# Megakernel on one core: weights loaded in order of use, x loaded turned, and a last stage that adds the two expert results on TensorE, takes its small statistics for two batches at once and holds four consecutive tokens per partition

## What is computed

```python
x = _layernorm(x + _L0_attn_ref(x, ...))   # state-space block: x @ W_in, conv over 4 taps, pw_kernel, 8-state scan
x = _layernorm(x + _L0_ffn_ref(x, w))      # x @ sign(w).T
x = _layernorm(x + _L1_attn_ref(x, ...))   # gated linear attention, 16 heads of 64
x = _layernorm(x + _L1_ffn_ref(x, ...))    # 8 experts, each token takes its best 2, hidden size 512
...
def _layernorm(x, axis=-1, eps=1e-05):
    m = jnp.mean(x, axis=axis, keepdims=True)
    v = jnp.var(x, axis=axis, keepdims=True)
    return (x - m) / jnp.sqrt(v + eps)
```

## Time and profile before

| | |
|---|---|
| median of 3 runs | 2472.59 us (2466.28 to 2479.43) |
| profiled execution: time, span | 2474.75 us, 2472.9 us |
| busy over the span | PE 85%, weight loads 63%, DVE 79%, ACT 58%, POOL 33% |
| 0 to 20 us | PE 0.00, DVE 2.01, ACT 1.28 us busy; DMA busy 0.84 |
| a round (521.3 to 636.4 us) | 115.1 us: PE 103.96, DVE 99.83, ACT 77.85, POOL 39.13 us busy; PE clock 1.00 |
| 2420 to 2440 us | PE 0, DVE 19.14, ACT 9.71, POOL 16.53 us busy; PE clock 0.50; DMA 0.81 busy, 229 GB/s |

### The profile page before, as it was taken

The page is one execution under the profiler, slowest core; times in us unless marked ns, Lnnn a source line. Parts: engine busy times, 40 slices in busy tenths (PEclk is TensorE's granted clock), DMA queues, the critical chain, the costliest instruction groups (busy, mean ns, idle before and its releaser), DMA issues. The chain is left out here.

```text
span 2472.9 us, 52605 instructions
## 1 busy us (share of the span) xinstructions
PE 2107.4 (85%) x15800; PEld 1560.8 (63%) x15929; DVE 1962.8 (79%) x3681; ACT 1427.6 (58%) x3256; POOL 808.0 (33%) x1060
## 2 busy tenths in 40 slices
PE   4389898989989898989898989899889849999980
PEld 1147565656657565657575656566566749999980
DVE  2787989798988888888988897989885447777768
ACT  2366766666667675666767666666655413333334
POOL 0111424141415141423324241414141333333337
PEclk9699999999999999999999999999989969999995
DMA  3452424152433324243424241524230042122117
GB/s 118 103 126 61 107 69 117 50 124 61 111 86 81 102 64 102 65 114 78 108 69 101 68 116 51 124 60 111 72 92 14 30 151 59 55 60 59 55 52 196
DMA packets 160526, 212.88 MB, mean 86 GB/s; under 512 B 20296, under 2 KB 97104, under 8 KB 160064
## 3 DMA queue, kind: packets, MB, share of 16 engines
q1 hardware_dynamic: 138192, 144.20, 19.7%
q0 software_dynamic: 22272, 67.92, 13.4%
HBM read 134.71 MB, written 28.08 MB: 66 GB/s over the span
## 5 line engine op out<-in xcount | busy, mean ns | idle before, releaser
L1432 DVE TENSOR_TENSOR_SCAN hs<-decay,push 128x512 f32<-128x512 f32 x256 | 320.1, 1272 | 7.1
L1184 ACT ACTIVATE S<-banks,fall_tok 128x128 f32<-128x128 f32 x1024 | 278.8, 385 | 27.7 <-PE banks L816 27.4
L1003 PE MATMUL banks<-rowsT,w_here 128*128 128x128 f32 x2176 | 269.6, 278 | 6.5 <-DVE w_here L1774 6.5
L1003 PEld LDWEIGHTS banks<-rowsT,w_here 128*128 128x128 f32 x2176 | 256.0, 193 | 10.1 <-issue 9.1
L1853 POOL DMA_DIRECT2D y<-ch x96 | 88.1, 918 | 477.2 <-DVE ch L1440 374.5
L1944 POOL TENSOR_TENSOR qd<-q,q_fall 128x512 f32<-128x512 f32 x96 | 159.4, 1660 | 208.7 <-ACT chunk_fall L1169 208.7
L1540 DVE TENSOR_TENSOR S<-banks,S 128x512 f32<-128x512 f32 x256 | 167.8, 683 | 64.2 <-PE banks L828 44.9
L1985 POOL DMA_INDIRECT results_scratch<-rows_out,result_to x136 | 132.2, 972 | 241.2 <-ACT rows_out L1310 234.5
L1425 DVE TENSOR_TENSOR push<-du,b_all 128x1024 f32<-128x1024 f32 x128 | 198.1, 1547 | 2.0 <-DMA b_all<-bc_scratch 2.0
L1299 ACT ACTIVATE tanh_h<-banks 128x512 f32<-128x512 f32 x136 | 81.3, 598 | 203.3 <-PE banks L1003 203.3
L1547 DVE SCALAR_TENSOR_TENSOR oT<-tog,banks 128x512 f32<-128x512 f32 x128 | 87.2, 681 | 136.0 <-ACT sq L1152 135.9
(11 more groups left out here) (221 smaller groups left out, 5096.5 us busy)
## 6 DMA issues: line engine op xcount, KB each, us to landing
y<-ch POOLq DMA_DIRECT2D x96, 512.0 KB, 5.5
b_all<-bc_scratch SPq DMA_DIRECT2D x128, 256.0 KB, 3.9
c_all<-bc_scratch SPq DMA_DIRECT2D x128, 256.0 KB, 3.6
q_fall<-fall_scratch SPq DMA_DIRECT2D x192, 128.0 KB, 3.3
rows_in<-rows_scratch SPq DMA_DIRECT2D x136, 66.0 KB
both<-results_scratch SPq DMA_DIRECT2D x32, 256.0 KB, 3.4
w<-w_dram SPq DMA_DIRECT2D x3, 2048.0 KB, 9.6
x_tok<-x_dram SPq DMA_DIRECT2D x16, 256.0 KB, 3.2
```

What stands on the lines that cost most here:

```text
L1003: mm = pe.matmul(bank_h[:, u % 2, n, here], w_here[:, u % 2, n, here], x, start=True, stop=True)
L1184: ins = nc.scalar.activation(S[:, g, here], bank[:, here], ACT.Exp, bias=fall_tok[:, head:head + 1])
L1432: nc.vector.tensor_tensor_scan(hs[:, h, :], decay[:, n % 2, h, :], push[:, h, :], 0.0, ALU.mult, ALU.add).then_inc(s_scan, 1)
```

## The change

1. The list of loads is split in three, each with a semaphore: `conv_loads` (w_inT, taps, pw), then `xT` of batch 0, then seven `front_loads`, then 23 others in the order of use. PE, ACT and DVE wait for each part where it is first used. The preparation of late weights moves on DVE from the start to round 0, behind the convolution's `u1` (`prepare_late`).
2. The tap products use two banks and two tiles in turn.
3. The host passes x turned as well. SP loads it straight into `xT`, once `z1` of the batch before has been multiplied; the transposes, the ACT copy, the tile `x_tok` and the bank use `xT` go, which leaves 97 uses in a round.
4. In the last stage PE adds the two results: two matmuls with the identity into bank `slot`; DVE adds `tokens` to that bank. POOL's addition goes. The seven small steps, the power and the shift are done once for two batches, on 128x8.
5. `tokens`, `both` and `out` hold four consecutive tokens per partition (2 KB runs in DRAM instead of four of 512 B).

```diff
-FRONT = {"xT": 0, "u0": 1, "u1": 2, "xdbl": 3, "dt0": 4, "dt1": 4, "z0": 6, "z1": 6}
+FRONT = {"u0": 1, "u1": 2, "xdbl": 3, "dt0": 4, "dt1": 4, "z0": 6, "z1": 6}
...
-        w_tap = S[:, 1, 2 * P:4 * P].rearrange("p (c n) -> p c n", c=HALVES)
+        w_tap = S[:, 3, :].rearrange("p (s c n) -> p s c n", s=2, c=HALVES)
...
+        tokens_dram = x3_scratch.rearrange("b (p c) d -> b p c d", p=P)
...
-        out_dram = out.rearrange("b (c p) d -> b p c d", p=P)
-        both_dram = results_dram[0:2 * B * T, :].rearrange("(r b c p) d -> r b p c d", r=2, b=B, p=P)
+        out_dram = out.rearrange("b (p c) d -> b p c d", p=P)
+        both_dram = results_dram[0:2 * B * T, :].rearrange("(r b p c) d -> r b p c d", r=2, b=B, p=P)
...
+            for dst, src in conv_loads:
+                sp.dma_start(dst, src).then_inc(s_w_first, 16)
+            sp.dma_start(xT[:, TAPS - 1:TAPS - 1 + T], a["xT"][0]).then_inc(s_x_loaded, 16)
+            for dst, src in front_loads:
+                sp.dma_start(dst, src).then_inc(s_w_front, 16)
...
-                        sp.wait_ge(ring.full_sem("xT"), ring.full_at("xT", n - 1))
-                    sp.dma_start(x_tok[:], x_dram[bass.ds(n, 1)].rearrange("b p c d -> (b p) c d")
-                                 ).then_inc(s_x_loaded, 16)
+                        sp.wait_ge(ring.full_sem("z1"), ring.full_at("z1", n - 1))
+                        sp.dma_start(xT[:, TAPS - 1:TAPS - 1 + T], a["xT"][bass.ds(n, 1)].rearrange("b d t -> (b d) t")
+                                     ).then_inc(s_x_loaded, 16)
...
-                    sp.wait_ge(s_mixed, b + 1)
+                    sp.wait_ge(s_summed, b + 1)
                     load_both(b + FINAL_SLOTS)
...
-                if t >= 1:
-                    pe.wait_ge(s_wconv, t)
+                if t >= 2:
+                    pe.wait_ge(s_wconv, t - 1)
...
+            for b in range(B):
+                slot = b % FINAL_SLOTS
+                after(pe, s_mixed, b - FINAL_SLOTS + 1)
+                pe.wait_ge(s_both[slot], 32 * (b // FINAL_SLOTS + 1))
+                for r in range(2):
+                    mm = pe.matmul(banks[:, slot, :], eye[:], both[:, slot, r].rearrange("p c d -> p (c d)"),
+                                   start=(r == 0), stop=(r == 1))
+                mm.then_inc(s_summed, 1)
...
-                dve.wait_ge(s_added, b + 1)
-                nc.vector.tensor_tensor(final_in[:, slot], both[:, slot, 0], both[:, slot, 1], ALU.add).then_inc(s_mixed, 1)
...
+                dve.wait_ge(s_summed, b + 1)
+                nc.vector.tensor_tensor(final_in[:, slot], banks[:, slot, :].rearrange("p (c d) -> p c d", d=P),
+                                        tokens[:, b * TILES:(b + 1) * TILES, :], ALU.add).then_inc(s_mixed, 1)
...
+            for m in range(B // 2):
+                mix_results(2 * m)
+                mix_results(2 * m + 1)
+                final_deviation(m)
```

More of the change, by code:

```diff
@@ L35 @@
 LN_STEPS = 11
+PAIR_STEPS = 15
 RMS_EPS = float(np.finfo(np.float32).eps)
@@ L311, in build @@
         ones = sb("ones", [P, P])
-        x_tok = sb("x_tok", [P, TILES, P])
         xT = sb("xT", [P, TAPS - 1 + T])
@@ L731, in turn, with convolve @@
                 mm.then_inc(full, 1)
-            def turn_input(n):
+            def convolve(h, n):
                 pe.wait_ge(s_x_loaded, at(n, 16, 16))
-                turn("xT", x_tok, n)
-            def convolve(h, n):
-                bank, full = fill(ring, f"u{h}", n, "xT")
+                bank, full = fill(ring, f"u{h}", n)
                 for t in range(TAPS):
@@ L965, in body @@
             def body(i, j, n):
+                if i is not None and first(i):
+                    pe.wait_ge(s_weights, WEIGHTS)
+                    pe.wait_ge(s_prep_late, PREPARED_LATE)
                 if j is not None:
@@ L1046, in _ @@
                 act.wait_ge(s_wmul, t + 1)
-                nc.scalar.activation(w_conv[:, t, :], ring_banks[:, 0, 0:2 * P], ACT.Copy, scale=0.5
+                nc.scalar.activation(w_conv[:, t, :], ring_banks[:, t % 2, 0:2 * P], ACT.Copy, scale=0.5
                                      ).then_inc(s_wconv, 1)
+            act.wait_ge(s_prep, PREPARED)
             def full(ring, use, it):
@@ L1053, in full @@
                 return ring.bank(use)
-            def turn_input(n):
-                nc.scalar.copy(xT[:, TAPS - 1:TAPS - 1 + T], full(ring, "xT", n)).then_inc(ring.free_sem("xT"), 1)
             def convolved(h, n):
@@ L1256, in body @@
             def body(i, j, n):
+                if i is not None and first(i):
+                    act.wait_ge(s_weights, WEIGHTS)
                 if j is not None:
@@ L1381, in _, with prepare_late @@
             dve.wait_ge(s_prep, PREPARED)
+            def prepare_late():
+                dve.wait_ge(s_weights, WEIGHTS)
+                for w in (w_out, w_k):
+                    nc.vector.tensor_scalar(w[:], w[:], 0.5, None, ALU.mult).then_inc(s_prep_late, 1)
+                for t in range(PAIRS):
+                    nc.vector.tensor_scalar(w_o[:, t, :], w_o[:, t, :], norm_w[:, t:t + 1], 0.5 * HID ** 0.5,
+                                            ALU.mult, ALU.mult).then_inc(s_prep_late, 1)
+                nc.vector.tensor_scalar(w_less, w_ffn[:], 0.0, None, ALU.is_lt).then_inc(s_sign, 1)
+                nc.vector.tensor_scalar(w_sign[:], w_ffn[:], 0.0, None, ALU.is_gt).then_inc(s_sign, 1)
+                dve.wait_ge(s_sign, 2)
+                nc.vector.tensor_tensor(w_sign[:], w_sign[:], w_less, ALU.subtract).then_inc(s_prep_late, 1)
+                nc.vector.tensor_scalar(x3_rows[:, :, TO], token_no[:], float(ALL_TOKENS - T), None, ALU.add
+                                        ).then_inc(s_token_no, 1)
+                dve.wait_ge(s_token_no, 1)
+                dve.wait_ge(s_prep_late, PREPARED_LATE)
             def full(ring, use, it):
@@ L1410, in normalize @@
                                             ALU.subtract, ALU.mult).then_inc(done, 1)
-            def layer_norm(x, step, scale, done, it):
-                deviation(x, step, it)
-                normalize(x, scale, done, it)
             def state_part(n, part, i):
@@ L1624, in stage @@
                             convolved(half, n)
+                    if h == FRONT["u1"] and first(n):
+                        prepare_late()
                 if i is not None:
@@ L2018, in _ @@
                     shares_of(t // MOE_LOAD + 1)
-            pool.wait_ge(s_tokens, 16 * B)
-            for b in range(2):
-                add_token(b)
-            for b in range(B):
-                final_shift(b)
-                if b + 2 < B:
-                    add_token(b + 2)
+            for m in range(B // 2):
+                final_shift(m)
 def kernel(**inputs):
```

115 lines of the change are left out of this document (52 added, 63 removed).

## The result

| | before | changed |
|---|---|---|
| median of the runs compared | 2467.91 us (5 runs, 2466.28 to 2479.43) | 2452.34 us (5 runs, 2446.38 to 2452.66) |
| ratio, 95% interval | | 0.9919 (0.9894 to 0.9944) |
| profiled execution, its span | 2474.75, 2472.9 us | 2452.34, 2450.4 us |
| first convolution starts | 35.20 us | 10.80 us |
| last stage (first load of `both` to the end of the span) | 2408.3 to 2472.9: 64.6 us | 2375.2 to 2450.4: 75.2 us |

The kernel is 0.8% faster. The forecast was 2457, the range 2444 to 2468. One execution and the next differ by some us, so I read the causes from the traces. Between the two profiled executions the time fell by 22.4 us. I read three points in time: the start of the last `x` load of the rounds, at 1752.98 before and 1723.96 now (-29.0); the first load of `both` (-33.1); the end (-22.4).

The account below looks back on a forecast made before the run. Bounds: the wait for all weight loads at the start, PE and DVE nearly full in rounds, DVE held up by POOL in the last stage. From 2472.59, -23.5 + 1.5 + 0 + 6.5 = -15.5 gives 2457 us, range 2444 to 2468.

Parts of the forecast that it names:

- The start: Before the first convolution: reordered loads and back-to-back tap products save 23.5 us, ends -21.0 and -24.5.
- Late weights: DVE's late weight preparation, moved behind `u1`, costs nothing, covered by 10.0 us of idling; 3.3 without cover.
- The boundary: Beginning of round 2: SP's wait for `z1` delays the load of b, +1.5 us, ends +0.5 and +2.2.
- The rounds: 14 full rounds: dropping the transposes gains 0, since PE waits for DVE behind them; at best -8.4 us.
- Rival (d): Rounds: each gives PE's 0.6 us back, -8.4 us, time 2449; chance 0.08.
- Rival (e): Rounds: b and c come late behind the `z1` wait in every round, 30 us slower, time 2487; chance 0.05.
- The last stage: Last stage: late loads, waiting for pairs and a cold PE make loops of 15.7 us per four batches, +6.5 us.
- its first sum takes 3.4, its second starts 1.75 late and takes 2.2: Last stage: PE begins each pair at the low clock, adding 1.75 + 0.3 us to a 13.6 us loop.
- Rival (a): Last stage: PE's clock, once up, stays up; loops of 13.6 us, stage +0.2, time 2451; chance 0.15.
- Rival (b): Last stage: PE stays at 1.2 GHz throughout; loops of 17.3 us, stage +15.5, time 2466; chance 0.17.
- Rival (c): Last stage: DVE binds, not the loads; 4.2 us a pair, stage -20, time 2431; chance 0.08.
- The sum: Whole kernel: -23.5 + 1.5 + 0 + 6.5 = -15.5 us, set against the median of 2472.59.

Follow-up runs that it names:

- PE kept busy: Changed kernel plus PE products nobody reads, four before the first sum and seven before batches 4, 8 and 12: 2446.65 us, last stage 71.1 us.
- stores later: Kernel with output stores issued by ScalarE, each store now behind the next batch's scalings, plus four unused PE products before the first sum: 2428.82 us.

## Why the prediction was right

- **The start**, forecast -23.5: measured -24.4 at the start of the convolution, and 1.5 more at its end (7.14 against 8.67 us), -25.9. The steps held, the sizes were too small: the convolution starts at 10.80, ahead of the 12 to 14.5 that I had named as a sign. The products got faster earlier than I had taken (5.31 us in all, where four of 2.05 are 8.2 and I had 6.3; the granted clock reads 1.00 all through the start in both traces, so only the durations tell this), and load 3 landed 2.7 us after its issue, not 3.4; the end of -24.5 was passed by 1.4, mostly for these two. The order of loads is shown as cause for 17.4 of it, x's turning for 1.6; the 5.4 of the tap products is the difference that is left.
- **Late weights**, forecast 0: right, but closer than I wrote. They landed at 25.0, not 21.5, DVE stood 5.0 for them and worked some 3, and of the 10.0 us of cover 1.93 is left, as 10.0 - 8 says.
- **The boundary**, forecast +1.5: wrong, 0. SP was late as predicted, but b reached DVE 3.8 us after its issue instead of 6.1, so DVE's wait went from 2.02 to 1.84, where I had named a longer one as a sign. I had assumed the same landing. Before, the loads of `x` and `x_tok` went out 0.98 and 0.55 us ahead of b; now `x` goes 3.06 ahead, and `xT` 0.37 ahead in longer runs. Which of the two shortened the landing no run separates. With x turned on PE b took 5.1 us and DVE waited 0.98; against that run the wait for `z1` costs 0.9, so the zero may be luck in part.
- **The rounds**, forecast 0: right within 0.2 us a round, by the run with x turned on PE. Rival (d) falls. Rival (e) too: the mean round did not grow, and in the middle rounds `xT` goes out 0.67 us behind the `x` load, as before. My sign of a middle round that changes by over 0.5 us was badly chosen: single rounds changed by -3.2 to +2.1 us, as they do between kernels with the same rounds.
- **The last stage**, forecast +6.5: right in mechanism, too small in size, +10.6. At 75.2 us it lies just past the 75 that I had named as a sign of a wrong prediction. The steps hold one by one: from DVE's addition for the second batch of a pair (2401.86) to ACT's end on that pair (2406.45 + 3.18 = 2409.63) it takes 7.8 us where I had 7.75; the power on 8 columns 1.64 for 1.6; no small step above 0.17; from the store of a group's first batch to the first sum on its load 3.9 (my sum had 3.97). The term that failed is "its first sum takes 3.4, its second starts 1.75 late and takes 2.2". The clock rises later than that: the two sums took until 2401.86 from 2395.15, 6.7 us instead of 5.6, which is 1.1 of the 1.4 us that a ring is too long. The first two pairs left ACT 17.5 and 21.4 us after the first load, for 17.4 and 21.5 forecast; with 2.5 for the last store 51.3 us are left for three rings, 17.1 each. Three times 17.1 - 15.7 are 4.2 us, the whole difference.
  The Trainium skill (DMA: Bandwidth & Descriptors, Anatomy of one DMA) would have made the landing 2.6 us, as an estimate, and the ring shorter still; its fit is for DMAs issued from GpSimd, and these are issued from SyncE. 2.6 is the shortest landing of `both` here, the median is 4.3.
- **Rival (a)**, the clock stays up once it has risen: not so in the changed kernel, but so in the runs in which PE's gaps were filled or closed. **Rival (b)**, low all the way, gave 17.3 a ring, which is nearer to the ring's length than my own value, though the clock did rise in each group. **Rival (c)**, DVE binds and not the loads, is near to what happens once the stores are off SP: DVE then takes the 2.1 us a batch that it said, but ScalarE with its stores sets the pace at 2.12, and the stage is 14.3 us shorter and not 20. The change as it is does not do this.
- **The sum** was -15.5 against the median, and the difference of medians is -15.6 here. That is luck, since the terms are not as close: the profiled pair differs by 22.4, of which -26.6 lies ahead of round 3 (forecast -22.0), +10.6 in the last stage, and -6.5 in rounds and the experts' stage between, where the code is the same but for x's turning and the forecast had 0. The last is within what executions differ by; no run shows its cause.

## What to carry to other kernels

When a stage's engines are relieved, look for the ring through the DMA queue. Here each load was issued behind a store that waited for its engine. That made load, work and store one closed loop, and what adds latency without adding work then lengthened it: doing two at a time cost 13.3 us, the slow clock 4.1 or more. With the stores on another sequencer's queue, doing two at a time cost nothing. Whether more slots than four would have opened the ring as well, no run tried. A gain that shows only when two edits come together is found by running each alone and both.

## What the runs showed of the hardware that I had not expected

- With a group of sums behind 6.8 us without work, the granted clock stood at 0.50 for about 6 us of nearly unbroken PE work (2395.15 to some 2401) before it read 1.00. Four unused products that end 2.2 us ahead of the first sum kept it at 1.00 in one run (PE kept busy) and not in another (stores later), where it fell to 0.50 after the sum had begun. Sums without gaps kept it at 1.00.
- Runs of 2 KB instead of 512 B cut the packets of the last stage by a factor of 3.7 and the landing of a 256 KB load by nothing (4.3 against 4.4 us). With the stores on ACT the first two loads of the stage landed in 2.6 and 2.8 us, and the median of the stage was 4.5, with windows of up to 393 GB/s.
- Kernels with the same code in start and rounds reach the last stage at 2366 to 2386 us, and one kernel, run on two chips, came to 2422 and 2433 us. A part of it is in the rounds: the middle ones last about 115.0, 116.8 or 118.3 us each, and which of the three a round takes changes from execution to execution. The cause stays open; it was not looked into. A change of a few us in one stage is better read from that stage than from the time.
